# Second layer's scan: the spreads of key and value run ahead, and VectorE takes the next tile's product between scan and weighting

## The reference, cut to what matters

```python
q = (x @ Wq.T).reshape(b, t, h, d)      # b = 8 sequences, t = 512, h = 16 heads, d = 8, as the kernel sees them
k = (x @ Wk.T).reshape(b, t, h, d)
v = (x @ Wv.T).reshape(b, t, h, d)
surprise = jax.nn.sigmoid(jnp.maximum(x @ Wm1.T + bm1, 0.0) @ Wm2.T + bm2)
decay = 1.0 - surprise
...
def step(state, inp):
    qt, kt, vt, dt, gt = inp
    state = state * dt[..., None, None] + gt[..., None, None] * (kt[..., :, None] * vt[..., None, :])
    yt = jnp.einsum('bhd,bhde->bhe', qt, state)
    return (state, yt)
_, ys = jax.lax.scan(step, state0, (qT, kT, vT, dT, gT))
```

## Time and profile before

| | us |
|---|---|
| median of 3 runs | 2822.38 (2815.88 to 2824.11) |
| the profiled execution | 2793.07 |
| its span | 2791.5 |
| TensorE matmul busy | 2073.0 (74%) |
| VectorE busy | 1835.0 (66%) |
| ScalarE busy | 1172.9 (42%) |
| GpSimd busy | 427.1 (15%) |

### The profile page before, as it was taken

One profiled execution on the slowest core, in us unless ns is written; L12 is line 12 of the kernel. 1 busy time (PEld: TensorE's weight loads), 2 busy tenths in 40 slices (PEclk: granted clock), 3 DMA queues, 4 the chain that ended last, 5 costly groups with the idle time before them and its releaser, 6 DMA issues. The chain is left out here.

```text
span 2791.5 us, 44094 instructions
## 1 busy us (share of the span) xinstructions
PE 2073.0 (74%) x15996; PEld 1059.0 (38%) x15996; DVE 1835.0 (66%) x2939; ACT 1172.9 (42%) x2401; POOL 427.1 (15%) x575
## 2 busy tenths in 40 slices
PE   4477777752346758888886976699869886888898
PEld 3011112431226732222324511298744433555554
DVE  6698887756773358878743478733356677766665
ACT  3699996320001116666672422233443302137433
POOL 3000000000281122222221044011460000000100
PEclk9688889875677969999996867699989988988899
DMA  7522110000054442223200000122121333200000
GB/s 283 110 37 43 26 23 0 15 10 0 30 192 125 145 93 37 50 42 51 40 10 11 1 28 30 36 85 83 45 58 58 92 110 94 77 7 1 22 1 31
DMA packets 146879, 155.36 MB, mean 56 GB/s; under 512 B 53148, under 2 KB 122458, under 8 KB 146706
## 3 DMA queue, kind: packets, MB, share of 16 engines
q1 hardware_dynamic: 130904, 117.69, 16.4%
q0 software_dynamic: 12928, 25.47, 3.6%
q10 hardware_dynamic: 2880, 9.96, 0.9%
HBM read 87.38 MB, written 68.55 MB: 56 GB/s over the span
## 5 line engine op out<-in xcount | busy, mean ns | idle before, releaser
L786 DVE TENSOR_REDUCE a_nmax<-a_first 128x2 f32<-128x1024 f32 x256 | 307.7, 1219 | 86.5 <-PE a_first L883 84.5
L381 ACT ACTIVATE a_E<-a_scores,a_nmax 128x512 f32<-128x512 f32 x512 | 343.3, 722 | 20.0 <-DVE a_nmax L340 19.6
L864 ACT ACTIVATE a_E<-a_scores 128x512 f32<-128x512 f32 x512 | 278.2, 597 | 157.9 <-PE a_scores L897 154.4
L340 DVE TENSOR_REDUCE a_nmax<-a_scores 128x2 f32<-128x1024 f32 x256 | 300.1, 1217 | 35.4 <-PE a_scores L398 34.1
L398 PE MATMUL a_scores<-a_Vh,a_Kh 48*128 48x512 bf16 x512 | 113.4, 460 | 133.7 <-ACT a_E L381 102.1
L897 PE MATMUL a_scores<-a_Qh,a_Kh 51*128 51x512 bf16 x512 | 142.8, 399 | 51.5 <-ACT a_E L864 40.6
L409 PE MATMUL a_out<-a_E,a_QS 128*32 128x512 f32 x1024 | 163.9, 719 | 2.4 <-DVE a_QS L350 2.2
L883 PE MATMUL a_first<-a_Kh,a_Qh 48*128 48x512 bf16 x512 | 121.7, 417 | 34.8 <-DVE a_nmax L786 23.9
L1885 PE MATMUL a_ps_q<-a_yT,a_selI 32*128 32x512 f32 x128 | 101.7, 885 | 57.5 <-DVE a_state L1943 40.3
L910 PE MATMUL a_out<-a_E,a_V 128*32 128x512 f32 x1024 | 142.2, 629 | 0.4 <-ACT a_OZ L850 0.2
L398 PEld LDWEIGHTS a_scores<-a_Vh,a_Kh 48*128 48x128 bf16 x512 | 24.7, 96 | 303.6 <-ACT a_E L381 220.1
(11 more groups left out here) (468 smaller groups left out, 4668.4 us busy)
## 6 DMA issues: line engine op xcount, KB each, us to landing
f_up<-in_L_up SPq DMA_DIRECT2D x32, 256.0 KB, 2.9
slots<-zeros ACTq DMA_DIRECT2D x12, 640.0 KB, 15.1
a_rows_k<-a_parts SPq DMA_DIRECT2D x16, 384.0 KB, 3.4
a_Kh<-a_rows_k SPq DMA_DIRECT2D x16, 384.0 KB, 5.9
a_Vh<-a_rows_v SPq DMA_DIRECT2D x16, 384.0 KB, 9.6
a_Qh<-a_rows_q SPq DMA_DIRECT2D x32, 192.0 KB, 4.7
a_Kh<-a_rows_k SPq DMA_DIRECT2D x32, 192.0 KB, 5.2
f_xe<-slots SPq DMA_DIRECT2D x40, 128.0 KB, 2.1
```

The costliest lines, as they stand in the source:

```text
L340: v.tensor_reduce(nmax[:, rd % 2, r1, :, q], ps_s[u % 3][:], AX.X, ALU.max, negate=True).then_inc(S["max_ready"], 1)
L381: m = a.activation(E[:, u % NE, x], ps_s[u % 3][:, x], ACT.Exp, bias=nmax[:, rd % 2, r1, x, q:q + 1], accum_out=Z[:, rd % 2, r1, x, q:q + 1])
L786: v.tensor_reduce(out, ps_f[u % 2][:], AX.X, ALU.max, negate=True).then_inc(S["max_ready"], 1)
L864: a.activation(E[:, u % NE, x], ps_s[x][:], ACT.Exp, scale=SCALE).then_inc(S["exp_ready"], 1)
```

## The change

The one group of four spreads becomes three pieces. The key's spread of tile `i + 2` and the value's of tile `i + 1` are issued behind query and decay of tile `i`, each with waits and a semaphore of its own (`k_spread`, `v_spread`). `a2_gk_e` gets a third buffer; `a2_ps_k` stays single. The key's weights are turned by three quarters instead of two, so that the four spreads that now stand together still take four different quarters of the rows. On VectorE the order of a tile becomes scan, product of the next tile, weighting; both drains go, and semaphores guard what they guarded.

```diff
-                def expand(b, n):
-                    i, t = b * NT + n, ORDER[n]
-                    if n == 0 and b >= GATED_EARLY:
-                        pe.wait_ge(S["gated"], b - GATED_EARLY + 1)
...
-                    for ps, src, sel, turn in ((ps_q[i % 2], mix["q"], selI, 0), (ps_v[i % 2], mix["v"], selJ, 1),
-                                               (ps_k, mix["gk"], selI, 2), (ps_d[i % 2], mix["keep"], selI, 3)):
...
+                def spread_k(i):
+                    if i >= ALL:
+                        return
+                    if i % NT == 0 and i // NT >= GATED_EARLY:
+                        pe.wait_ge(S["gated"], i // NT - GATED_EARLY + 1)
                     if i:
                         pe.wait_ge(S["k_read"], i)
+                    spread(ps_k, "gk", selI, i, 3).then_inc(S["k_spread"], 1)
+
+                def spread_v(i):
+                    if i >= ALL:
+                        return
                     if i >= 2:
                         pe.wait_ge(S["kv_done"], i - 1)
+                    spread(ps_v[i % 2], "v", selJ, i, 1).then_inc(S["v_spread"], 1)
+
+                def spread_dq(i):
+                    if i >= 2:
                         pe.wait_ge(S["scanned"], i - 1)
                         pe.wait_ge(S["state_ready"], i - 1)
...
+                    spread(ps_q[i % 2], "q", selI, i, 0)
+                    spread(ps_d[i % 2], "keep", selI, i, 3).then_inc(S["expanded"], 1)
...
+                spread_k(0)
+                spread_v(0)
                 for b in range(NB):
                     for n in range(NT):
-                        expand(b, n)
+                        spread_dq(b * NT + n)
+                        if b * NT + n == 0:
+                            spread_k(1)
+                        spread_v(b * NT + n + 1)
+                        spread_k(b * NT + n + 2)
...
-                    a.wait_ge(S["expanded"], i + 1)
-                    if i >= 2:
-                        a.wait_ge(S["kv_done"], i - 1)
-                    a.copy(gk_e[:, i % 2], ps_k[:]).then_inc(S["k_read"], 1)
+                    a.wait_ge(S["k_spread"], i + 1)
+                    if i >= 3:
+                        a.wait_ge(S["kv_done"], i - 2)
+                    a.copy(gk_e[:, i % 3], ps_k[:]).then_inc(S["k_read"], 1)
...
+                def scan(i):
+                    v.wait_ge(S["expanded"], i + 1)
+                    v.wait_ge(S["kv_done"], i + 1)
+                    if i >= NT:
                         v.wait_ge(S["picked"], i // 4 - 1)
...
+                product(0)
+                for i in range(ALL):
+                    b, n = i // NT, i % NT
+                    scan(i)
+                    if i + 1 < ALL:
+                        product(i + 1)
+                    weigh(i)
+                    if n == 3 and GATED_EARLY <= b + 1 < NB:
+                        gated(b + 1)
...
-    a["L2_W"] = np.stack([a["L2_attn_Wk"].T[:, turned[2]], a["L2_attn_Wv"].T[:, turned[1]], a["L2_attn_Wq"].T], axis=1)
+    a["L2_W"] = np.stack([a["L2_attn_Wk"].T[:, turned[3]], a["L2_attn_Wv"].T[:, turned[1]], a["L2_attn_Wq"].T], axis=1)
```

More of the change, by code:

```diff
@@ L1854, in scan2 @@
     NT = len(ORDER)
+    ALL = NB * NT
     ctx = ExitStack()
@@ L1858, in scan2 @@
         selI, selJ, pick = mix["selI"], mix["selJ"], mix["pick"]
-        gk_e, kv = (k.sb(f"a2_{n}", [128, 2, T]) for n in ("gk_e", "kv"))
+        gk_e, kv = k.sb("a2_gk_e", [128, 3, T]), k.sb("a2_kv", [128, 2, T])
         state = k.sb("a2_state", [128, NT, T])
@@ L1865, in scan2 @@
         ps_y = k.ps("a2_ps_y", [128, T])
-        S = {n: g.sem(f"a2_{n}") for n in ("gated", "expanded", "k_read", "kv_done", "scanned", "state_ready", "picked",
+        S = {n: g.sem(f"a2_{n}") for n in ("gated", "k_spread", "v_spread", "expanded", "k_read", "kv_done", "scanned", "state_ready", "picked",
                                            "y_read")}
@@ L1933, in product, with weigh @@
                     v.wait_ge(S["k_read"], i + 1)
-                    v.tensor_tensor(kv[:, i % 2], gk_e[:, i % 2], ps_v[i % 2][:], ALU.mult).then_inc(S["kv_done"], 1)
-                def run(b, n):
-                    i = b * NT + n
-                    if b:
+                    v.wait_ge(S["v_spread"], i + 1)
+                    if i >= 2:
+                        v.wait_ge(S["scanned"], i - 1)
+                    v.tensor_tensor(kv[:, i % 2], gk_e[:, i % 3], ps_v[i % 2][:], ALU.mult).then_inc(S["kv_done"], 1)
+                def scan(i):
+                    v.wait_ge(S["expanded"], i + 1)
+                    v.wait_ge(S["kv_done"], i + 1)
+                    if i >= NT:
                         v.wait_ge(S["picked"], i // 4 - 1)
-                    v.tensor_tensor_scan(state[:, n], ps_d[i % 2][:], kv[:, i % 2], 0.0, ALU.mult, ALU.add
+                    v.tensor_tensor_scan(state[:, i % NT], ps_d[i % 2][:], kv[:, i % 2], 0.0, ALU.mult, ALU.add
                                          ).then_inc(S["scanned"], 1)
-                    v.drain()
-                    v.tensor_tensor(state[:, n], state[:, n], ps_q[i % 2][:], ALU.mult).then_inc(S["state_ready"], 1)
-                for b in range(NB):
-                    for n in range(NT):
-                        product(b * NT + n)
-                        v.drain()
-                        run(b, n)
-                        if n == 3 and GATED_EARLY <= b + 1 < NB:
-                            gated(b + 1)
+                def weigh(i):
+                    v.wait_ge(S["scanned"], i + 1)
+                    v.tensor_tensor(state[:, i % NT], state[:, i % NT], ps_q[i % 2][:], ALU.mult
+                                    ).then_inc(S["state_ready"], 1)
+                product(0)
[7 more added lines that the diff above has]
+                        gated(b + 1)
             @block.gpsimd
@@ L3400, in layout @@
     turned = [(np.arange(C) - 32 * n) % C for n in range(4)]
-    a["L2_W"] = np.stack([a["L2_attn_Wk"].T[:, turned[2]], a["L2_attn_Wv"].T[:, turned[1]], a["L2_attn_Wq"].T], axis=1)
+    a["L2_W"] = np.stack([a["L2_attn_Wk"].T[:, turned[3]], a["L2_attn_Wv"].T[:, turned[1]], a["L2_attn_Wq"].T], axis=1)
     a["L2_Wm1"] = a["L2_attn_Wm1"].T
     a["L2_bm1"] = a["L2_attn_bm1"].reshape(32, 1)
-    a["L2_Wm2"] = np.stack([a["L2_attn_Wm2"].T[:, turned[n] // HD] for n in (2, 3)], axis=1)
-    a["L2_bm2"] = np.stack([a["L2_attn_bm2"][turned[n] // HD] for n in (2, 3)], axis=1)
+    a["L2_Wm2"] = np.stack([a["L2_attn_Wm2"].T[:, turned[n] // HD] for n in (3, 3)], axis=1)
+    a["L2_bm2"] = np.stack([a["L2_attn_bm2"][turned[n] // HD] for n in (3, 3)], axis=1)
     row = np.arange(128)
```

7 lines of the change are left out of this document (4 added, 3 removed).

## The result

| | before | changed |
|---|---|---|
| median of 20 runs each, us | 2810.30 | 2784.36 |
| ratio, 95% interval | | 0.9904 (0.9885 to 0.9923) |
| the profiled execution, us | 2793.07 | 2771.55 |
| its span, us | 2791.5 | 2770.0 |
| first to last scan, us | 185.5 | 162.8 |

A forecast was written before the change was run, and what follows sets the result against it. The scan was taken as bound by VectorE's 2.71 us step plus 12.4 us of ring waits. Gain 35.0 - 15.0 (low clock) - 0.4 (edges) = 19.6 us, from 2822.4 to 2802.8 us; range 2786 to 2817.

The forecast's parts named there:

- The reference: Whole kernel: the 19.6 us gain is taken from the median of 2822.38 us, giving 2802.8 us.
- Part 1: VectorE in the scan: without drains a step falls from 2.71 to 2.35 us, gaining 35.0 us if the others keep up.
- The added waits: VectorE's new semaphore waits (`v_spread`, `scanned`, `kv_done`) cost between 0 and 0.05 us a step.
- Part 2: Scan at the high clock: the key's spread-and-copy ring of 1.89 us stays under 2.35 us, so the cost is 0.
- Part 3: Scan at the low clock: 19 tiles (30%) take 3.14 us each, 0.79 us over a high one, costing 15.0 us.
- The sums behind a late key: Column sums on TensorE at the low clock: waiting for the key's spread hides nothing, 3.32 us a tile instead of 3.14.
- Part 4: Edges of the scan: the first decay's spread stands behind the first key's in the same 32 rows, 0.4 us once.
- The clock stays high: Rival for the scan: all 63 steps at 2.35 us, gain 34.6 us, 2787.8 us; chance 15%.
- the low share doesn't change: Rival for the scan: 58% stays at the low clock, 35 tiles cost 28 us, gain 7 us, 2815 us; chance 10%.
- Neighbours not shortened: Rival on VectorE: neighbouring instructions don't overlap, a step of 2.59 us, 2814 us; chance 8%.
- Slower: the clock stays low: Rival at the key's spread, copy and sums: 63 steps of 3.14 us, 14.7 us slower, 2837 us; chance 6%.
- the order takes the lead away: Rival at TensorE's in-order queue: VectorE waits in every tile, 2.85 us or more a step, 2819 us; chance 3%.

The follow-up runs named there:

- the two experiments with drains: TensorE's new program with VectorE's old order and both drains: ratio 0.9999, 2792.39 us; the changed kernel with a drain after each VectorE instruction: 2823.25 us.
- VectorE's part alone: VectorE's new order without drains, on TensorE's and ScalarE's program of the kernel before: ratio 1.0232, 2861.44 against 2795.84 us.
- the second execution: The changed kernel profiled a second time, nothing altered: span 2776.4 us, first to last scan 160.4 us.
- each half alone: Only VectorE's new order, or only TensorE's and ScalarE's new program, against the kernel before: ratios 1.0232 and 0.9999.

## Why the prediction was wrong

The direction and the mechanism were right, and so were the signs that it named: scans 2.31 us apart in most of the stretch, a granted clock of 0.82 (over 0.80), a profiled span of 2770.0 us (about 2772). The time, 2784.4 us, lies 1.6 us under the range (2786 to 2817) and 18.4 us under the forecast. Point by point:

- **The reference: the step that failed by most.** "The 19.6 us are taken from the median", 2822.38. That median was of 3 runs, and all 20 of the same kernel gave 2810.3. 12.1 of the 18.4 us are this. Four series of the kernel before, of 7 to 20 runs, have medians from 2795.5 to 2810.3, and by the last table an execution is uncertain by some 20 us outside the scan; the range had no term for it. From 2810.3 the same gain would have given 2790.7, inside the range, so which runs came first decided here between right and wrong. The other 6.3 us are gain: 3.1 in the scan (below), and 3.2 outside it, whose cause stays open and which may be scatter.
- **Part 1, VectorE's step.** Predicted 2.35 with a lower bound of 2.33, measured 2.31. All pairs are shortened, as taken; a dependent pair is not (1.25 us behind the last scan of 1.22). But the product is shorter too (0.662 instead of 0.683 us), which I held constant, and starts are 1.13, 0.58 and 0.60 apart instead of 1.14, 0.60 and 0.61. 63 x 0.04 = 2.5 us, outside my bound of 2.33, for which the prediction shows no row. "The added waits cost 0 to 0.05 us": it is 0; they cost something where several stand behind a drain (the two experiments with drains).
- **Part 2, the high clock.** Right: of 38 steps at the high clock the median is VectorE's own 2.31. That it was the lead that did this is shown by VectorE's part alone, 3.25 us.
- **Part 3, the low clock.** The size is nearly exact, by luck, since the make-up is wrong. Predicted 15.0 us, 19 tiles at 0.79; measured 14.9 us with the edges, at a low share of 35% (30% in the second execution). A low tile takes 2.75 us (I had 2.85), and one with sums at its end 4.4 to 4.7. Three of the first and one of the second make 3.17 to 3.24 us each, between my 3.14 and the 3.32 without any cover. What I hadn't seen is that a lone low tile costs next to nothing (2.31 to 2.35 us); the lead covers it. Nearly half of the loss is the start, where the clock is low for 20 us on end, and the rest are the sums. Two errors cancelled.
- **The sums behind a late key.** By the Trainium skill's rule on the mode switch (TensorEngine Tiling, Key Properties) the sums wait for the late key's spread, the 3.32 us. In the rows above the value's spread ends at 1713.89 + 1.06 = 1714.95, the key's at 1714.40 + 1.06 = 1715.46, and the sums start at 1715.39, though their own semaphore was raised long before. So they did wait for the key, some 0.5 us beyond its neighbours. The trace agrees with the rule but doesn't prove it: the sums take all rows, the key's 32 among them, and would queue behind it for that alone.
- **Part 4, the edges.** "0.4 us once" was wrong in size and in reason. The first decay's spread is over before the first scan, so it isn't in the steps at all. The first step is 5.42 us, 2.7 us over a plain low one. 1.7 of these are the second query behind a key of the same rows, and the scan waits for it because the semaphore of the later decay is raised in program order. All of it is inside the 14.9 us above.
- **The rivals.** "The clock stays high" (2787.8) is nearest in time, but not what happened: it was low for a third of the stretch, and not for the 58% of "the low share doesn't change" either. "Neighbours not shortened" is out by the 2.31. "Slower: the clock stays low" and "the order takes the lead away" are out; the first has its likeness in VectorE's part alone, where the lead is missing.

The sum with measured terms: 185.5 - (145.5 + 2.4 + 14.9) = 22.7 us in the scan of the two profiled executions, against 19.6 predicted, and 2.5 of the missing 3.1 us are the step.

## What to carry to other kernels

Reordering a chain on one engine, so that independent instructions stand between dependent ones, pays only if the engines that feed it get the lead that the new order asks for: here each half alone gave 0 or cost 65 us, and together they gave 27 us. A drain is cheap with at most one semaphore wait behind it and dearer with more. One semaphore for a group of products waits for the slowest one ahead in the program; placing the wanted one first took 1.7 us off the one step where this showed, though the whole scan didn't gain by it. A prediction of a gain should carry the scatter of the whole kernel's time, read from more than three runs, beside the bounds of the gain.

## What the runs showed of the hardware

- VectorE: two independent instructions of 128 x 512 float32 start closer than their own length: 1.13 us behind a scan of 1.22, 0.58 behind a product of 0.66, 0.60 behind a weighting of 0.68. A dependent one, held by a semaphore, starts 1.25 us behind the scan, and 1.32 with a drain. An explicit drain makes the next instruction start 0.09 us behind the end of the last one with at most one semaphore wait between, 0.16 with two and 0.19 with three, even if the targets were reached long ago.
- TensorE: products in different quarters of the rows pass each other in their starts (decay 1609.88, query 1611.74, against the program), but the semaphore of the later one is raised only once the earlier one is done, 1.7 us after its own end.
- The clock: the same sums in halves, twice as often, took the granted clock over the scans from 0.82 to 0.94, and superfluous products from 0.82 to 0.92; but with the key's spread in the query's rows TensorE was busy 171.5 of 177.9 us at 0.75. Before, the scan took 185.4 to 185.5 us in three executions, each with 58% at the low clock, though in one of them the high and low stretches fell elsewhere.
